# Queries read from the kept x_t, context of the first two pairs loaded ahead of the fetches, and half of the shared expert's second layer placed behind the expert blocks

## The reference, cut to what matters

```python
x = L0(x, ctx, mask0, mask1)    # self attn, cross attn, feed-forward, layer norms   phases 0, 1
x = L1(x, ctx, mask2, mask1)    # self attn, cross attn, experts                     phases 2, 3
x = L2(x, ctx, ctx, mask4)      # cross attn, layer norm                             phase 4
x = L3(x, ctx, ctx)             # cross attn, feed-forward                           phase 5

def moe_ffn(x, gate_w, exp_w1, exp_w2, sh_w1, sh_w2):    # inside L1, after phase 3
    sh = silu(xf @ sh_w1.T) @ sh_w2.T                    # the shared expert, all 2048 tokens
    topk_vals, topk_idx = top_k(xf @ gate_w.T, 2)
    gates = softmax(topk_vals) scattered to 8 experts
    sel = sum over the two chosen experts of gate * (silu(xf @ w1[e].T) @ w2[e].T)
    return sh + sel
```

## Time and profile before

| | before |
|---|---|
| median of 3 runs | 751.35 us (750.5 to 751.66) |
| the profiled execution | 758.92 us, its span 757.1 us |
| mean granted TensorE clock | 0.953 of full speed |
| PE busy | 685.2 us, 91% of the span |
| DVE, ACT, POOL busy | 532.5, 449.6, 317.3 us |
| DMA | 47.25 MB, mean 62 GB/s |

### The profile page before, as it was taken

The page is one execution under the profiler, slowest core; times in us unless marked ns, Lnnn a source line. Parts: engine busy times, 40 slices in busy tenths (PEclk is TensorE's granted clock), DMA queues, the critical chain, the costliest instruction groups (busy, mean ns, idle before and its releaser), DMA issues.

```text
span 757.1 us, 26752 instructions
## 1 busy us (share of the span) xinstructions
PE 685.2 (91%) x9408; PEld 468.5 (62%) x9408; DVE 532.5 (70%) x1306; ACT 449.6 (59%) x1242; POOL 317.3 (42%) x523
## 2 busy tenths in 40 slices
PE   1999999999999999999997688999974889999996
PEld 1566666777777666666665366777752456666764
DVE  0599899798998888788886331444431589998884
ACT  1477777777767777777665322434321567677884
POOL 2244444466666533333775630433442154443110
PEclk9999999999999999999997599999995699999998
DMA  8333434222432311111110001112105011111110
GB/s 255 101 90 93 99 91 99 64 68 62 106 111 84 90 44 31 44 40 38 55 41 19 31 27 25 45 53 56 47 28 146 26 30 43 31 33 34 47 41 26
DMA packets 60047, 47.25 MB, mean 62 GB/s; under 512 B 7834, under 2 KB 54430, under 8 KB 58801
## 3 DMA queue, kind: packets, MB, share of 16 engines
q1 hardware_dynamic: 53152, 28.57, 13.5%
q10 hardware_dynamic: 4528, 13.18, 7.2%
q0 software_dynamic: 2272, 4.24, 1.7%
HBM read 25.34 MB, written 14.79 MB: 53 GB/s over the span
## 4 chain that ended last, share of the span: by engine, by line
PE 79%; issue 8%; DVE 5%; ACT 4%; DMA 2%; ACTq 1%; POOL 1%; SPq 0%; DVEq 0%; POOLq 0%
PE ps L565 14%; PE ps L602 12%; PE ps L735 6%; PE ps L795 5%; PE ps L805 5%; PE ps L743 5%; PE ps L655 4%; PE ps L677 4%; PE ps L643 4%; PE ps L716 3%; PE ps L763 2%; PE ps L815 2%; PE ps L587 2%; PE ps L656 2%; PE ps L773 2%
## 5 line engine op out<-in xcount | busy, mean ns | idle before, releaser
L1088 DVE TENSOR_REDUCE top<-ps 128x16 f32<-128x1024 f32 (+1 forms) x96 | 108.8, 1133 | 42.3 <-PE ps L565 41.2
L495 POOL TENSOR_TENSOR k_by_j<-k_t,cst 128x512 f32<-128x512 f32 (+1 forms) x96 | 95.4, 994 | 81.2 <-ACT k_t L912 44.8
L487 POOL TENSOR_TENSOR rstd<-spread,half_neg 128x1 f32<-128x1 f32 x80 | 44.7, 558 | 194.5 <-DVE spread L1181 111.9
L565 PE MATMUL ps<-k_by_j,q_t 32*64 32x256 f32 (+1 forms) x1536 | 124.3, 394 | 1.3 <-issue 0.2
L602 PE MATMUL ps<-cst,prob 128*128 128x128 f32 x704 | 119.8, 291 | 1.2 <-ACT prob L933 1.0
L602 PEld LDWEIGHTS ps<-cst,prob 128*128 128x128 f32 x704 | 76.8, 143 | 61.3 <-issue 44.8
L1104 DVE TENSOR_TENSOR prob<-ps,top 128x1024 f32<-128x1024 f32 (+1 forms) x96 | 108.3, 1128 | 0.7
L933 ACT ACTIVATE prob<-prob 128x1024 f32<-128x1024 f32 (+1 forms) x96 | 94.8, 987 | 22.2 <-DVE prob L1104 22.1
L1054 DVE RECIPROCAL inv<-ps 128x128 f32<-128x128 f32 x96 | 91.7, 955 | 18.6 <-PE ps L743 17.6
L882 ACT ACTIVATE prob_t<-ps 128x512 f32<-128x512 f32 (+1 forms) x96 | 53.9, 562 | 44.9 <-PE ps L602 44.6
L524 POOL DMA_INDIRECT expert_out<-rows_out,rows_in x39 | 38.3, 983 | 85.3 <-DVE rows_out L1269 85.3
(11 more groups left out here) (157 smaller groups left out, 1270.8 us busy)
## 6 DMA issues: line engine op xcount, KB each, us to landing
sorted_rows<-zero_rows ACTq DMA_DIRECT2D x32, 276.2 KB, 2.7
stage_m<-in_m SPq DMA_DIRECT2D x80, 64.0 KB
stage_x<-x_t SPq DMA_DIRECT2D x80, 64.0 KB
mow<-in_mow SPq DMA_DIRECT2D x18, 256.0 KB, 3.0
stage_kv<-in_ctx_t SPq DMA_DIRECT2D x64, 64.0 KB
rows_in<-sorted_rows SPq DMA_DIRECT2D x39, 65.0 KB
wat<-in_wat ACTq DMA_DIRECT2D x1, 1280.0 KB, 7.6
stage_x<-in_x_t SPq DMA_DIRECT2D x16, 64.0 KB
```

The lines of the kernel that those rows point to most:

```text
L495: pool.tensor_tensor(k_by_j[:, p, 0:nj, :], k_t[:, p:p + 1, :].broadcast_to([128, nj, TOK]), cst[:, cj:cj + nj].unsqueeze(2).broadcast_to( ...
L565: mm = pe.matmul(ps[S * b:S * b + S, 2 * p + bank, r * nj * S:(r + 1) * nj * S].rearrange("p (h k) -> p h k", k=S), q_t[rows_g, p, S * b:S ...
L1088: dve.tensor_reduce(top[:, p, 0:nh].rearrange("p (b h) -> p b h", b=2), sc, AX.X, ALU.max).then_inc(top_d, 1)
```

## The change

1. **Queries from `x_t`.** `stage_x` is gone. In phase 0, SP loads the pair from DRAM straight into its place in `x_t`; in the other phases there is no DMA for the queries. PE's query projection reads `x_t` and waits itself for what made it: the feed-forward's semaphore `f_xt` in phase 2, `c_xt` in phase 4, `xt_e` otherwise. In the loops the address of `x_t` is in a register.
2. **First two pairs of phase 4.** Their context and mask are loaded behind SP's `blocks()` and ahead of its fetches, and no longer wait for `c_xt`.
3. **Shared expert.** `shared_out(2)`, `shared_out(3)` on PE and `shared(2)`, `shared(3)` on DVE run behind `blocks()`. PE's blocks wait for `s_res` of 2 and not of 4. `shared_h` must now outlive the blocks, so `got` becomes a view of the experts' first-layer weights in `mow1`.

```diff
-        stage_x = sb("stage_x", [128, 2, TOK])
...
-        got = shared_h[:, :, :, :].rearrange("p a c t -> p (a c t)").rearrange("p (n i d) -> p n i d", i=NP, n=2)
+        got = mow1[:, 1:1 + E, :].rearrange("p e h -> p (e h)").rearrange("p (n i d) -> p n i d", i=NP, n=2)
...
-                if ph == FF + 1:
-                    sp.wait_ge(f_xt, i + 1 if isinstance(i, int) else NP)
-                elif ph == RO + 1:
-                    sp.wait_ge(c_xt, i // 2 + 1 if isinstance(i, int) else NP // 2)
-                wait_pair(sp, proj_d, pr, 2)
+                kept = x_t[:, bass.ds(i * TOK, TOK)]
                 if ph == 0:
-                    tok = a["x_t"][bass.ds(i, 1), :, :].rearrange("a p t -> p (a t)")
+                    src = a["x_t"][bass.ds(i, 1), :, :].rearrange("a p t -> p (a t)")
+                    wait_pair(sp, proj_d, pr, 2)
+                    sp.dma_start(kept, src).then_inc(ld_x[p], 16)
+                elif SELF[ph]:
+                    if ph == FF + 1:
+                        sp.wait_ge(f_xt, i + 1 if isinstance(i, int) else NP)
+                    src = kept
                 else:
-                    tok = x_t[:, bass.ds(i * TOK, TOK)]
-                sp.dma_start(stage_x[:, p, :], tok).then_inc(ld_x[p], 16)
-                src = tok if SELF[ph] else a["ctx_t"][bass.ds(i, 1), :, :].rearrange("a p t -> p (a t)")
+                    src = a["ctx_t"][bass.ds(i, 1), :, :].rearrange("a p t -> p (a t)")
...
             def slot(at):
                 pr = at(OFF_PROJ)
-                if pr is not None:
+                if pr is not None and not (pr.phase == RO + 1 and isinstance(pr.i, int) and pr.i < 2):
                     load(pr)
...
             blocks()
+            for i in range(2):
+                load(Pair(RO + 1, i, 0, i))
             for k in range(NP // 2):
                 fetch(k)
...
-                    pe.wait_ge(ld_x[p], 16 * (pr.half + 1))
+                    if ph == 0:
+                        pe.wait_ge(ld_x[p], 16 * (pr.half + 1))
+                    elif ph == FF + 1:
+                        wait_own(pe, f_xt, pr)
+                    elif ph == RO + 1:
+                        pe.wait_ge(c_xt, pr.i // 2 + 1 if isinstance(pr.i, int) else NP // 2)
+                    else:
+                        wait_pair(pe, xt_e, pr, NP)
                     pe.wait_ge(ld_kv[p], 16 * (pr.half + 1))
...
-                    pe.matmul(ps[:, B_PROJ, 0:128], wat[:, ph, 0, :], stage_x[:, p, :], start=True, stop=True)
+                    pe.matmul(ps[:, B_PROJ, 0:128], wat[:, ph, 0, :], x_t[:, bass.ds(pr.i * TOK, TOK)], start=True, stop=True)
...
-                pe.wait_ge(s_res, NT)
+                pe.wait_ge(s_res, 2)
...
             shared_in(3)
+            blocks()
             shared_out(2)
             shared_out(3)
-            blocks()
             back(0)
...
             shared(1)
+            blocks()
             shared(2)
             shared(3)
-            blocks()
```

## The result

| | before | after |
|---|---|---|
| median | 751.5 us (4 runs, 750.5 to 752.35) | 739.77 us (4 runs, 739.46 to 740.74) |
| ratio | | 0.9843, 95% interval 0.982 to 0.9866 |
| profiled execution | 758.92 us, span 757.1 | 739.72 us, span 737.8 |
| mean granted clock | 0.953 | 0.970 |

The change saves 11.7 us between the medians (10.1 to 13.5 by the interval). The forecast was 739.7 us. The two profiled executions differ by 19.2 us, which is more than the medians do.

A forecast was written before the change was run, and what follows sets the result against it. PE held 79% of the chain, DMA 2%, so only PE's waits, chiefly between last block and phase 4, counted. 7.24 + 3.97 + 0.4 = 11.6 us off the 751.35 us median gave 739.7 us; range 735 to 744.5.

The forecast's parts named there:

- Front side: Shared expert to first block: with tiles 2 and 3 gone from there, the first block starts 7.24 us earlier.
- Back side: Last block to phase 4's first projection: early context and unstaged queries gain 3.97 us net, 1.84 us loss included.
- the prediction's clock term: Phase 4's start: low clock as before, but back(0) and perhaps part of a projection at the high level; 0.4 us gain.
- Against the fetched data, which still lands at T + 6.26: Behind the blocks: fetched expert results still arrive 6.26 us after the last block's end (T), as before.
- The loss of 1.84 us: Behind the blocks: DVE's last shared add holds combine(0) until T + 8.1 instead of T + 6.26.
- Context not the limit: Phase 4's start, rival: something else holds the first projection, so the back side gives nothing; 743.7 us, chance 0.13.
- Pair 2: no wait, at most 1 us: Phase 4: pair 2's context, still behind the fetches, lands in time; at most 1 us wait if the clock were high.
- one of the signs that I named for being wrong: Wrong if looped phases' slots grow, PE waits for pair 2's context, or phase 4's start has a high clock.
- Address instructions: Ahead of the query projection in 38 looped pairs: cost 0; bound 0.06 us each, 2.3 us in all.
- The dip at the blocks' start: Start of the blocks: the same dip to clock 0.50 as before expected, after a PE gap of 1.65 us.
- The shared expert at the low level behind the blocks: Behind the blocks, rival: a clock drop makes the moved 7.3 us up to twice that; 747 us, chance 0.05.
- The rival that it stays high: Phase 4's start: clock stays high because PE's idle time is filled, 4 us shorter; 735.7 us, chance 0.12.

The follow-up runs named there:

- e1_part3: Kernel before with only the shared expert's tiles 2 and 3 moved behind the blocks; 747.27 us, ratio 0.9949.
- e0: Kernel before, run and profiled once more with no edit; 751.59 us, ratio 1.0009.
- e2_parts12: Changed kernel with the shared expert's tiles 2 and 3 back ahead of the blocks; 746.44 us, ratio 0.9934.
- e6_combine_first: Changed kernel with DVE's combine(0) ahead of shared(3), waiting for the first tile's add alone; 738.76 us, ratio 0.9834.
- e3: Kernel before with only the queries read from x_t, no stage_x; 750.42 us, ratio 0.9991.
- e4: Kernel before with context and mask of phase 4's first two pairs loaded ahead of the fetches, queries still staged; 750.49 us, ratio 1.0004.
- e5: Changed kernel without the early context and mask loads of phase 4's first two pairs; 746.03 us, ratio 0.9936.
- e7_fill: Changed kernel with 54 extra matmuls, computing nothing needed, in PE's gaps around phase 4's start; 735.95 us, ratio 0.9811.
- e12_best: Changed kernel with combine(0) ahead of shared(3), SP's fetches 4 to 7 later, 36 filling matmuls, 40 tiny early matmuls; 732.9 us, ratio 0.9749.

## Why the prediction was right

- **Front side, 7.24 us.** Measured 8.89 - 1.63 = 7.26, the transpose 1.63 us after the first layer's last matmul (predicted 1.65). e1_part3 has the same 1.60. Right. The profile names "issue" where I wrote ACT: the silu ended at 449.98 + 0.60 = 450.58, and the 0.99 us from there to the transpose is the wait's and the expert number's, as taken from the earlier trace rows.
- **Back side, net 3.97 us.** The first query projection went from T + 14.22 to T + 9.90, 4.32 us, and from e0's T + 13.90, 4.00 us. `combine(0)` at T + 8.05 (predicted 8.1), `back(0)` at T + 8.99 (9.0). The 0.35 us beyond 3.97 are mostly the prediction's clock term: `back(0)` took 0.44 us at the high level and not 0.69. Without the shared halves e2_parts12 gave 5.3 us where I had 5.8.
- **"Against the fetched data, which still lands at T + 6.26": wrong, and without effect on the sum.** In the changed kernel the fetches are issued 1.5 us later, behind a code fetch, and the data releases `combine(0)` at the last moment: 0.17 us of wait. That it cost nothing is luck: the delay of 1.5 us fell into the 1.84 us for which the add held `combine(0)` in any case. The loss of 1.84 us has two causes nearly equally late, the add and the data. Removing one alone (e6_combine_first) brings `combine(0)` forward by 0.37 us. I had priced the code's place in memory at nothing, because no row of before shows it.
- **Context not the limit (rival, 0.13): refuted.** e3, e4 and e5 wait 5.99 to 6.09 us for whichever load stays behind the fetches. It also shows that my reason for this rival was half right: x's own copy was queued there too, and would have held the projection alone.
- **Pair 2: no wait, at most 1 us.** It waited 0.73 us; 1.39 in e7_fill, where the start is faster. Mis-sized by 0.7 us, inside the bound. A wait of PE there was one of the signs that I named for being wrong, and it came: this step failed, in a size too small to move the sum. I had let it land 2.3 us after issue, but from 562.14 to the projection at 566.85 were 4.71 us, with the fetches, issued 1.5 us later than I had them, still running beside it (share 1.18 at 561 to 562).
- **Address instructions: 0.** L696's slots are 7.57 us apart as before. e3_part1, which has them, is at 0.9991. No row shows the 0.06 us that my bound put on each; the upper end of e3_part1's interval, 1.0006, leaves 0.45 us for all 38, unless the saved traffic paid for them.
- **The dip at the blocks' start: did not come.** I had it as unchanged. The clock is at 1.00 at 454 in the kernel after and at 461 in e0_before_again. It belonged to the first profiled execution, whose blocks took 99.86 us and not 98.5. So my premise that a gap of 1.74 us is enough for a drop does not hold either: one execution shows it, another one with the same gap does not. The sum had nothing on it.
- **The shared expert at the low level behind the blocks (rival, 0.05): refuted.** The 64 matmuls start at 549.91 and take 7.31 us as before, with the clock at 1.00 in each window from 550 to 560.
- **Clock, 0.4 us.** The low level from T + 11 for 20 us, as forecast, though from a premise that did not hold (see the dip at the blocks' start). The rival that it stays high was priced at 4 us. When fillers brought it about, e7_fill gave 3.2 us within K0 to K6 and e12_best 5.7, so the size was about right (e12_best has other edits in it as well), and the change alone did not bring it about. My argument against it was one window with PE busy throughout at 0.50. The rows of these kernels are of two kinds. In the one after, PE is busy throughout 580 to 581 at 0.50 still, and has no work at all at 571 to 572. In e7_fill, with the gaps filled, the level is 1.00 at 565, 0.50 at 567 and 1.00 again by 570. The Trainium skill (TensorE: Matmul & The Clock Gate, Part 1: The HAM clock gate) has sustained matmul activity release the throttle. e7_fill agrees with it. Whether the start of phase 4 in the kernel after is such activity, the busy shares, whose ends are modelled, can't tell.
- **The baseline.** I took the savings over unscaled onto the median, 7.57 us below the profiled time. e0_before_again confirms that the excess belonged to that execution and lay nearly all outside the places changed. Had I summed from the profiled time, the forecast would have been 7.6 us too high; scaling the savings would have changed it by 0.1.

What stays open: the parts do not add in the medians (3.8 + 5.0 = 8.8 of 11.8 us) although they nearly do in the landmarks (5.9 + 5.3 = 11.2). The intervals (2.6 to 5.0, 3.2 to 6.8, 10.1 to 13.5) allow for that difference. Runs of before spread over 748.8 to 755.6 us, and the drain ahead of the shared expert takes 31.1 to 34.8 us from profile to profile. A single profile of each kernel can't say how often the longer one occurs in which.

## What to carry to other kernels

When two loads stand behind the same long transfer, removing either gains nothing: list everything that is queued there before you price one of them (e3 and e4 0, both 5 us). Work put into a wait pays only up to what else is late: here the add and the fetched data ended 0.17 us apart, so look at the second releaser, and move the cheap item ahead. And take a second profile of the kernel before where its time is 1% off the median. Here it would have shown at once which 7 us were no part of the question, and that the dip at the blocks' start was not the kernel's.

## What the runs showed of the hardware that was not expected

- Instructions are fetched by DMA during the execution, by the queues' name in the page: the kernel after has

```profile
q8 instruction: 58, 0.95, 0.6%
```

  that is 16 KB a packet in q8. One that falls on an indirect scatter holds one DMA engine for about 1.2 us, and the scatter lands 3.7 us after its issue (2.1 in e4_part2_staged, where none falls on it). The fetches behind it start 1.1 to 1.8 us late. 40 tiny matmuls early in the program moved it away.
- PE's gap of 1.48 us ahead of `back(0)` was followed by the low level by T + 10.9, while after a gap of 0.36 us it came at T + 17, in a stretch without PE work. In K0 to K6 the two kernels differ by 2.2 us, twice the 1.1 us by which the data was late. That gap and clock hang together is open: at the blocks' start a gap of 1.74 us was followed by the low level in one execution of before, and one of 1.75 us was not in another.
- A 64 KB load issued behind the 2 MB of fetches held PE until 4.5 to 6.7 us after its issue (4.45 in e0_before_again, 5.54 in e4_part2_staged, 6.41 in e5_parts13, 6.71 in e3_part1), where a row block of 65 KB ahead of the first block lands after 2.3.
